# Moving two of four PSUM evictions from ScalarE to VectorE, and moving once-a-batch stages to other slots, in a causal attention kernel

## The chip, the cores and the metric

The kernel runs on 1 core of one Trainium2 chip. The metric is device time in microseconds (us) of the whole program. The kernel before takes 3825.32 us, the median of 3 runs (3816.24 to 3826.53).

## The reference

```python
x = L0_attn_x                                   # 8 x 512 x 128, float32
h = _layernorm(x) * (1 + ca) + sa               # per-batch modulation
x = x + ga * attn(h)                            # 16 heads of 8, 512 tokens, rope, causal softmax
h = _layernorm(x) * (1 + cb) + sb
x = x + gb * ffn_stack(h)                       # 6 layers: windowed attention + gated FFN

# attn(h):
q, k, v = heads(x @ Wq.T), heads(x @ Wk.T), heads(x @ Wv.T)
q, k = _apply_rope(q, k, cos, sin)
scores = einsum('bhqd,bhkd->bhqk', q, k) / sqrt(8) + causal_mask
out = einsum('bhqk,bhkd->bhqd', softmax(scores), v)
return out.reshape(B, S, 128) @ Wo.T
```

The change is in the causal attention, the first part of the program ("the causal half", `part_a` in the code). The 6-layer stack behind it (`part_b`) and the output (`part_c`) are the same in both kernels, and start when the causal half has ended.

## The kernel before, in words

The causal half works through 8 batches. A batch has 16 heads, taken in 4 groups of 4, so there are 32 groups. In each group, the queries and keys of the 4 heads are laid out on 128 partitions, 32 partitions to a head (8 rows in use for the head, two float32r parts of each, and in row 0 of the block the constant one of `one`, which lets a product add the row maximum).

Each engine's program is written as a loop over slots `s`, and each stage of the work is given a slot number: TensorE does the fills of stage X at slot X_AT (+11 per group, or +44 per batch), and the engine that empties the bank does it at X_AT+1 or later. A group has 11 slots (`PER`), a batch 44. All engines run through the slots in the same order, but each waits only for the semaphores of the instruction that comes next, so the order within a slot and the distance in slots between a producer and its consumer set who waits for whom. In each slot TensorE does:

- the fills of the general bank of that slot: there are 2 such banks, `gen0` and `gen1`, used in turn by all stages together, in the order of the list `gen_order`. `begin` (L360 on) makes a fill wait until the fill but one before it has been emptied. The stages of every group are stackq, stackk, stack2 (4 heads' queries, keys, and queries with their maximum), turn and back (the output turned, and the denominators turned back). In places modulo 11 they are at 3, 5, 2, 9 and 4. The stages that come once a batch are h (normed input turned), q, qr, k, kr (projections, plain and rotated), v, y (output projection), yt and h2. In places modulo 44 they are at 5, 10, 12, 13, 15, 20, 31, 34 and 43; so h shares a slot with stackk, k with stack2, kr with back, v and y with turn.
- one step of `scores` (L420, L421): scores by query into one of 3 banks `tm`. VectorE takes their negated row maximum (L737). The step of slot s waits (`need(pe, max_d, u - 2)`) until the maximum of slot s-3 has been taken.
- one step of `scores_by_key` (L435, L437), for a group 16 slots before, into one of 2 banks `km`. ScalarE takes the exponential (L587). The step waits for the exponential of two slots before.
- at four of eleven places one `weigh` (L451), which multiplies the exponentials with the values into `po`. ScalarE copies `po` to `oT` (L578) at place 7, and turn at place 9 reads it.

The stack of keys (stackk, place 5) is emptied in four pieces of 32 partitions (L549), one per head, each into its own column block of `kG` (3 of these homes). All four are done by ScalarE, one in each slot at the places 6, 7, 8 and 9, ahead of that slot's exponential. Only the fourth counts up `g_act`, which is what the scores of the next group (place 0) wait for and what the fill after next in the banks `gen` waits for.

VectorE multiplies q, qr, k, kr with the rope tables (L699) one slot after each fill, takes the maxima, takes part in turn, back and yt, and does two layernorms per batch: "h" in five parts at the places 40, 42, 44, 46, 48 of the batch, and "h2" in five parts at 35 to 39. Each of these parts stands ahead of the maximum of its slot. GpSimd adds the rope halves (L602) and takes the low parts (L607).

Of the kernel before, what the change touches and what calls it, by code (L numbers as in the profile page):

```python
# [193 lines left out]
    return g if r == 0 and 0 <= g < NG else None  # L194


H_AT, Q_AT, QR_AT, K_AT, KR_AT, V_AT = -39, -34, -32, -31, -29, -24
STACKQ_AT, STACKK_AT, STACK2_AT, TURN_AT, BACK_AT = -8, -6, 13, 31, 37
WEIGH_AFTER = 1
Q_HOMES, K_HOMES = 2, 3  # L200
Y_AT, YT_AT, H2_AT = 75, 78, 87


def gen_order():
# [31 lines left out]
def part_a(nc, t_in, alloc, need, x_attended, resT, ident, masks, mod, vecs):  # L236
# [3 lines left out]
    with ctx:  # L240
        sb, ps, sem = alloc(ctx)
# [10 lines left out]
        one = sb("one", [P, 1])  # L252
# [38 lines left out]
        mod_p = sem("mod_p"); mod_e = sem("mod_e"); mod_d = sem("mod_d"); sel_d = sem("sel_d")  # L291
        rot_w = sem("rot_w"); vec_e = sem("vec_e"); vec_z = sem("vec_z"); clear_d = sem("clear_d"); clear_k = sem("clear_k"); wo_p = sem("wo_p"); wo_d = sem("wo_d")
        st = sem("st"); passed = sem("passed"); rstd_d = sem("rstd_d"); nrm = sem("nrm"); ahead_d = sem("ahead_d"); after_d = sem("after_d")
        g_fill = sem("g_fill"); g_act = sem("g_act"); g_dve = sem("g_dve")
        rope_a = sem("rope_a"); hi_d = sem("hi_d"); lo_d = sem("lo_d")
        tm_full = sem("tm_full"); max_d = sem("max_d"); km_full = sem("km_full"); exp_d = sem("exp_d")
        w_done = sem("w_done"); o_out = sem("o_out"); wide_d = sem("wide_d")
# [34 lines left out]
        def _(pe):  # L332
# [25 lines left out]
            def begin(name, k):  # L358

                i = GEN[name, k]  # L360
                if i >= 2:
                    user = GEN_LIST[i - 2]
                    if user[0] in BY_VECTOR:
                        pe.wait_ge(g_dve, GEN_DVE[user] + 1)
                    else:
                        pe.wait_ge(g_act, GEN_ACT[user] + 1)
                return gen[i % 2]

            def four_turns(bank, src):
# [40 lines left out]
            def scores(u):  # L410

                gr, i = divmod(u, PER)
                j, hh, n = ROWS[i]
                if i == 0:
                    pe.wait_ge(g_act, GEN_ACT["stackk", gr] + 1)
                need(pe, max_d, u - 2)
                pe.sem_inc(pe_passed, 1)
                width = (j + 1) * P
                bank = tm[u % 3][:, 0:n * width].rearrange("p (h w) -> p h w", h=n)
                nc.tensor.matmul(bank, qG[:, gr % Q_HOMES, j * P:width], kG[:, gr % K_HOMES, hh:hh + n, 0:width], start=True, stop=False)  # L420
                nc.tensor.matmul(bank[:, :, j * P:width], ident_r, causal_mask.rearrange("p (o k) -> p o k", o=1).broadcast_to(  # L421
                    [P, n, P]), start=False, stop=True).then_inc(tm_full, 1)
# [86 lines left out]
        @block.scalar  # L509
        def _(act):  # L510
            act.wait_ge(tr_w, 1)
            nc.scalar.activation(wT[:, 0:4, :], tm[0][:, :].rearrange("p (i f) -> p i f", i=4), ACT.Copy).then_inc(ev_w, 1)
            nc.scalar.activation(cT[:, :], tm[1][:, 0:BATCH], ACT.Silu).then_inc(silu_d, 1)
            act.wait_ge(loaded, NLOAD)
            nc.scalar.activation(sel[:, :, :], sel_raw[:, :, :], ACT.Copy).then_inc(sel_d, 1)
            nc.scalar.activation(mask_r[:, :], masks[:, 2 * KEYS:2 * KEYS + 3 * P], ACT.Copy).then_inc(sel_d, 1)
            act.wait_ge(wo_p, 1)
            nc.scalar.activation(wo_rows[:, :, :], tm[0][:, :].rearrange("p (i f) -> p i f", i=4), ACT.Copy).then_inc(wo_d, 1)
            act.wait_ge(clear_d, 3)

            def filled(name, k):
                act.wait_ge(g_fill, GEN[name, k] + 1)
                return gbank(name, k)

            for s in A_SLOTS:
                b = batch_at(s, H_AT + 1)
                if b is not None:
                    bank = filled("h", b)
                    act.wait_ge(ahead_d, b + 1)
                    nc.scalar.activation(hT[:, :], bank[:, :], ACT.Identity, bias=ahead_mod[:, 0:1],  # L530
                                         scale=ahead_mod[:, 1:2]).then_inc(g_act, 1)
                b = batch_at(s, V_AT + 1)
                if b is not None:
                    bank = filled("v", b)
                    need(act, w_done, 16 * (b - 1))
                    nc.scalar.activation(values[:, b % 2, :, :, 0:A_HDIM], bank[:, :].rearrange(
                        "p (t h d) -> p t h d", t=TILES, h=A_HEADS), ACT.Copy).then_inc(g_act, 1)
                gr = group_at(s, STACKQ_AT + 1)
                if gr is not None:
                    bank = filled("stackq", gr)  # L540
                    nc.scalar.activation(qG[:, gr % Q_HOMES, :], bank[:, :], ACT.Copy).then_inc(g_act, 1)
                for hh in range(4):
                    gr = group_at(s, STACKK_AT + 1 + hh)
                    if gr is not None:
                        bank = filled("stackk", gr)
                        if gr < K_HOMES:
                            act.wait_ge(clear_k, gr + 1)
                        r = slice(32 * hh, 32 * hh + 32)
                        last = nc.scalar.activation(kG[r, gr % K_HOMES, hh, :], bank[r, :], ACT.Identity, bias=one[r, 0:1])  # L549
                        if hh == 3:  # L550
                            last.then_inc(g_act, 1)
                gr = group_at(s, STACK2_AT + 1)
                if gr is not None:
                    bank = filled("stack2", gr)
                    nc.scalar.activation(q2[:, gr % 2, :], bank[:, :], ACT.Copy).then_inc(g_act, 1)
                b = batch_at(s, Y_AT + 1)
                if b is not None:
                    bank = filled("y", b)
                    act.wait_ge(after_d, b + 1)
                    nc.scalar.activation(yT[:, :], bank[:, :], ACT.Copy, scale=after_mod[:, 0:1]).then_inc(g_act, 1)  # L560
                b = batch_at(s, H2_AT + 1)
                if b is not None:
                    bank = filled("h2", b)
                    nc.scalar.activation(resT[:, b, :], bank[:, :], ACT.Identity, bias=after_mod[:, 1:2],
                                         scale=after_mod[:, 2:3]).then_inc(g_act, 1)
                for c, off in ((0, Q_AT + 5), (1, K_AT + 5)):
                    b = batch_at(s, off)
                    if b is not None:
                        act.wait_ge(rope_a, 2 * b + c + 1)
                        if b >= 2:  # L570
                            act.wait_ge(g_fill, GEN["stack2", GROUPS * (b - 1) - 1] + 1)
                        nc.scalar.activation(qk_hi[:, b % 2, c, :], rot1[:, c, :], ACT.Copy).then_inc(hi_d, 1)
                gr = group_at(s, LAG + PER + WEIGH_AFTER + 1)
                if gr is not None:
                    act.wait_ge(w_done, 4 * gr + 4)
                    if gr >= 2:
                        act.wait_ge(g_dve, GEN_DVE["back", gr - 2] + 1)
                    nc.scalar.activation(oT[:, gr % 2, :], po[:, :], ACT.Copy).then_inc(o_out, 1)  # L578
                u = s - LAG
                if 0 <= u < NU:  # L580
                    gr, i = divmod(u, PER)
                    k, hh, n = KEYED[i]
                    if hh == 0:
                        need(act, w_done, 4 * gr + k - 2)
                    act.wait_ge(km_full, u + 1)
                    width = TOKENS - k * P
                    nc.scalar.activation(probT[:, (4 * gr + k) % 3, hh:hh + n, 0:width],  # L587
                                         km[u % 2][:, 0:n * width].rearrange("p (h w) -> p h w", h=n), ACT.Exp).then_inc(exp_d, 1)

        @block.gpsimd  # L590
        def _(pool):
# [5 lines left out]
            for s in A_SLOTS:  # L597
                for c, off in ((0, QR_AT + 2), (1, KR_AT + 2)):
                    b = batch_at(s, off)
                    if b is not None:  # L600
                        pool.wait_ge(g_dve, GEN_DVE[("qr", "kr")[c], b] + 1)
                        nc.gpsimd.tensor_tensor(rot1[:, c, :], rot1[:, c, :], rot2[:, c, :], ALU.add).then_inc(rope_a, 1)  # L602
                for c, off in ((0, Q_AT + 6), (1, K_AT + 6)):
                    b = batch_at(s, off)
                    if b is not None:
                        pool.wait_ge(hi_d, 2 * b + c + 1)
                        nc.gpsimd.tensor_tensor(qk_lo[:, b % 2, c, :], rot1[:, c, :], qk_hi[:, b % 2, c, :].bitcast(f32),  # L607
                                                ALU.subtract).then_inc(lo_d, 1)
# [9 lines left out]
        def _(dve):  # L618
# [64 lines left out]
            for s in A_SLOTS:  # L683
# [10 lines left out]
                for c, r, off in ((0, 0, Q_AT), (0, 1, QR_AT), (1, 0, K_AT), (1, 1, KR_AT)):  # L694
                    b = batch_at(s, off + 1)
                    if b is not None:
                        bank = filled(("q", "qr", "k", "kr")[2 * c + r], b)
                        need(dve, lo_d, 2 * (b - 1) + c + 1)
                        nc.vector.tensor_tensor((rot1, rot2)[r][:, c, :], bank[:, :], rope[:, 2 * c + r, :],  # L699
                                                ALU.mult).then_inc(g_dve, 1)  # L700
                gr = group_at(s, TURN_AT + 1)
                if gr is not None:
                    bank = filled("turn", gr)
# [827 lines left out]
```

## Time and profile before

| | |
|---|---|
| median of 3 runs | 3825.32 us |
| the profiled execution: its own time, its span | 3833.82 us, 3832.0 us |
| causal half, setup (0 to 49 us) | TensorE busy 18.25 us |
| causal half, loop (49 to 660 us) | 611 us; busy TensorE 542.35, VectorE 309.24, ScalarE 349.43, GpSimd 55.49 us |
| tail of the causal half (660 to 673 us) | 13 us |
| 6-layer stack and output (673 to 3832 us) | 3159 us |

The span is the time from the first to the last instruction of one profiled execution; the time of that execution has 1.82 us around it. Busy times are the union of an engine's instructions in a stretch. "Idle before" an instruction is the time its engine stood still, and the arrow names what ended the wait. PEclk is the TensorE clock that the chip granted: 1.00 is 2.4 GHz, 0.50 is 1.2 GHz.

### The profile page before, as it was taken

To read this page: it belongs to the slowest core of one execution; us is meant where nothing else is said; L and a number is where in the kernel's file an instruction comes from. 1 tells how busy PE (TensorE), PEld (TensorE's weight loads), DVE (VectorE), ACT (ScalarE), POOL (GpSimd) and SP (SyncE) were. 2 spreads that over 40 slices of the span, in tenths; PEclk is the share of its full clock that TensorE was granted. 3 is DMA by queue.
4 is the path that set the end of the run, shared out by engine and by line. 5 is a ranking of instruction groups with operands and counts; after the bars stand their busy time and mean duration, and the time that the engine had idled before them with its cause. 6 is when DMAs were issued, how large, how long until landed. Compare 5 with 4: busy or idle time off the path is not lost. (4 is left out here: it accounts for less than half of the span.)

```text
span 3832.0 us, 147280 instructions
## 1 busy us (share of the span) xinstructions
PE 3621.4 (95%) x64322; PEld 2756.7 (72%) x64322; DVE 3100.3 (81%) x4927; ACT 2455.5 (64%) x3855; POOL 2310.7 (60%) x1367
## 2 busy tenths in 40 slices
PE   6888888599999999999999999999999999999996
PEld 4666665477777777777777777777777777777774
DVE  4554454699988899989899989988899998889893
ACT  4555555367666667666667666666666766666663
POOL 1001000677777677777677777776777777777771
PEclk9999999799999999999999999999999999999998
DMA  1000000222222222222222222212222222221112
GB/s 56 4 4 4 4 7 7 64 54 56 54 56 54 68 54 56 54 56 60 61 54 56 54 63 62 56 53 56 54 68 54 56 54 54 57 57 52 52 52 70
DMA packets 122998, 188.79 MB, mean 49 GB/s; under 512 B 25054, under 2 KB 44278, under 8 KB 122108
## 3 DMA queue, kind: packets, MB, share of 16 engines
q1 hardware_dynamic: 122364, 179.36, 17.3%
q8 instruction: 517, 8.47, 0.9%
q14 instruction: 117, 0.96, 0.1%
HBM read 24.08 MB, written 4.19 MB: 7 GB/s over the span
## 5 line engine op out<-in xcount | busy, mean ns | idle before, releaser
L1308 POOL TENSOR_TENSOR rc<-rc,rnorm 128x1024 f32<-128x1024 f32 x384 | 731.4, 1905 | 394.5 <-DVE rnorm L170 377.4
L1302 POOL TENSOR_TENSOR rc<-rc,rs 128x1024 f32<-128x1024 f32 x384 | 910.6, 2371 | 7.2 <-DVE rs L1367 3.6
L1343 POOL TENSOR_TENSOR prob_b<-prob_b,rinv 128x1024 f32<-128x1024 f32 x192 | 365.4, 1903 | 358.3 <-DVE rinv L1448 358.2
L1361 DVE TENSOR_TENSOR rc<-proj,rope_b 128x1024 f32<-128x1024 f32 x384 | 465.6, 1212 | 87.1 <-ACT squares L1165 85.9
L1165 ACT ACTIVATE squares<-proj 128x1024 f32<-128x1024 f32 x384 | 392.7, 1023 | 181.5 <-PE proj L917 178.0
L1008 PEld LDWEIGHTS ring<-pT,vmoved 64*64 64x64 f32 x18432 | 380.3, 135 | 136.1 <-issue 136.1
L1367 DVE TENSOR_TENSOR rs<-proj,rope_b 128x1024 f32<-128x1024 f32 x384 | 466.1, 1214 | 0.0
L1375 DVE TENSOR_REDUCE sums<-squares 128x16 f32<-128x1024 f32 x384 | 463.9, 1208 | 0.0
L954 PEld LDWEIGHTS ring<-ident,rc 128*128 128x128 f32 x3072 | 361.5, 141 | 138.9 <-issue 43.5
L737 DVE TENSOR_REDUCE negmax<-tm 128x1 f32<-128x384 f32 (+3 forms) x352 | 222.3, 639 | 285.3 <-PE tm L421 285.0
L954 PE MATMUL ring<-ident,rc 128*128 128x128 f32 x3072 | 428.7, 277 | 12.2 <-POOL rc L1308 9.7
L1008 PE MATMUL ring<-pT,vmoved 64*64 64x32 f32 x18432 | 404.8, 221 | 25.2 <-issue 23.6
L1008 PE MATMUL ring<-pT,vown 64*64 64x32 f32 x6144 | 378.2, 220 | 6.1 <-issue 6.1
L1156 ACT ACTIVATE qT<-ring 128x512 f32<-128x512 f32 x384 | 228.3, 595 | 204.9 <-PE ring L954 204.9
L915 PE MATMUL proj<-wqkv_hi,xa_hi 128*128 128x512 f32 x768 | 330.3, 430 | 28.2 <-POOL xa_lo L1284 21.5
L1023 PE MATMUL proj<-oT_b,wo 128*128 128x256 f32 x1536 | 351.8, 383 | 2.0 <-issue 2.0
L587 ACT ACTIVATE probT<-km 128x512 f32<-128x512 f32 (+1 forms) x352 | 195.1, 557 | 241.7 <-PE km L437 236.5
L1156 ACT ACTIVATE vown<-ring 128x512 f32<-128x512 f32 x384 | 229.4, 598 | 178.2 <-PE ring L917 168.0
L1008 PEld LDWEIGHTS ring<-pT,vown 64*64 64x64 f32 x6144 | 332.5, 135 | 6.8 <-issue 6.8
L1156 ACT ACTIVATE pT<-ring 128x512 f32<-128x512 f32 x384 | 218.4, 595 | 183.7 <-PE ring L987 182.6
L974 PE MATMUL scr<-kT,qT 64*32 64x64 f32 x24576 | 332.8, 224 | 1.6 <-issue 1.3
L1156 ACT ACTIVATE kT<-ring 128x512 f32<-128x512 f32 x384 | 228.6, 595 | 157.6 <-PE ring L954 157.5
(172 smaller groups left out, 8027.4 us busy)
## 6 DMA issues: line engine op xcount, KB each, us to landing
vmoved<-vown SPq DMA_DIRECT2D x576, 128.0 KB
vmoved<-vown SPq DMA_DIRECT2D x192, 192.0 KB
vmoved<-vown SPq DMA_DIRECT2D x576, 64.0 KB
wqkv_raw<-in_L_ffn_Wqkv SPq DMA_DIRECT2D x40, 192.0 KB, 3.4
wo<-in_L_ffn_Wo SPq DMA_DIRECT2D x6, 512.0 KB, 4.8
x_attended<-xtok SPq DMA_DIRECT2D x8, 256.0 KB, 2.0
xtok_c<-x_attended SPq DMA_DIRECT2D x8, 256.0 KB, 4.4
out<-xtok_c SPq DMA_DIRECT2D x8, 256.0 KB, 2.8
```

Source lines behind the costliest of these rows:

```text
L954: last = nc.tensor.transpose(bank[:, p * P:(p + 1) * P], rc[:, k % 2, c, o:o + P], ident[:, :])
L974: last = nc.tensor.matmul(scr[32 * w:32 * w + 32, s, p, :], qT[rows, p, 32 * w:32 * w + 32], kT[rows, p, j * P + 32 * w:j * P + 32 * w + K ...
L1008: last[i] = nc.tensor.matmul(banks[i][64 * b:64 * b + 64, p, 32 * odd:32 * odd + 32], v[64 * s:64 * s + 64, :], pT[64 * s:64 * s + 64, p, ...
L1023: last = nc.tensor.matmul(bank[:, HALVES[half]], wo[:, p, :], oT[:, p, HALVES[half]], start=(p == 0), stop=(p == PAIRS - 1))
L1156: nc.scalar.activation(dst, src, ACT.Copy).then_inc(ring_free, 1)
L1165: nc.scalar.activation(squares[:, c, :], proj[c][:, :], ACT.Square).then_inc(sq_done, 1)
L1302: nc.gpsimd.tensor_tensor(rc[:, k % 2, c, :], rc[:, k % 2, c, :], rs[:, c, :], ALU.add).then_inc(add_done, 1)
L1308: nc.gpsimd.tensor_tensor(dst, dst, rnorm[:, k % 2, c * HEADS:(c + 1) * HEADS].rearrange("p (h o) -> p h o", o=1).broadcast_to([P, HEADS, ...
L1343: nc.gpsimd.tensor_tensor(pr, pr, rinv[:, :, :].rearrange("p q (s o) -> p q s o", o=1).broadcast_to([P, PAIRS, 2, KEYS]), ALU.mult).then_i ...
L1361: nc.vector.tensor_tensor(rc[:, k % 2, c, :].rearrange("p (h d) -> p h d", h=HEADS), proj[c][:, :].rearrange("p (h d) -> p h d", h=HEADS), ...
L1367: nc.vector.tensor_tensor(rs[:, c, :].rearrange("p (h s d) -> p h s d", h=HEADS, s=2), src[:, :, ::-1, :], tab.broadcast_to([P, HEADS, 2, ...
L1375: nc.vector.tensor_reduce(sums[:, c * HEADS:(c + 1) * HEADS], squares[:, c, :].rearrange("p (h d) -> p h d", h=HEADS), AX.X, ALU.add).then ...
```

## The change

Three things are changed. First, ScalarE does only the first two of the four evictions of a stack of keys, at the places 6 and 7; VectorE does the other two at the same places, as a `tensor_scalar` that adds the per-partition scalar `one`, and counts a semaphore of its own, `k_half`. Whoever waited for ScalarE's fourth eviction now waits for ScalarE's second and for `k_half`. Second, the batch stages get other slots: h from place 5 to 7, qr from 12 to 11, k from 13 to 12, kr from 15 to 18, v from 20 to 21, y from 31 to 32. None of them is in a slot with a stage of the groups any more. Third, the steps that follow the rotation are counted from the rotated projection: the high part (L572) goes from 15 and 18 to 14 and 21, the low part (L607) from 16 and 19 to 15 and 22.

```diff
-H_AT, Q_AT, QR_AT, K_AT, KR_AT, V_AT = -39, -34, -32, -31, -29, -24
+H_AT, Q_AT, QR_AT, K_AT, KR_AT, V_AT = -37, -34, -33, -32, -26, -23
...
-Y_AT, YT_AT, H2_AT = 75, 78, 87
+Y_AT, YT_AT, H2_AT = 76, 78, 87
...
                     else:
                         pe.wait_ge(g_act, GEN_ACT[user] + 1)
+                    if user[0] == "stackk":
+                        pe.wait_ge(k_half, 2 * user[1] + 2)
...
                 if i == 0:
                     pe.wait_ge(g_act, GEN_ACT["stackk", gr] + 1)
+                    pe.wait_ge(k_half, 2 * gr + 2)
...
-                for hh in range(4):
+                for hh in range(2):
                     gr = group_at(s, STACKK_AT + 1 + hh)
...
-                        if hh == 3:
+                        if hh == 1:
                             last.then_inc(g_act, 1)
...
-                for c, off in ((0, Q_AT + 5), (1, K_AT + 5)):
+                for c, off in ((0, QR_AT + 3), (1, KR_AT + 3)):
...
-                for c, off in ((0, Q_AT + 6), (1, K_AT + 6)):
+                for c, off in ((0, QR_AT + 4), (1, KR_AT + 4)):
...
+                for hh in (2, 3):
+                    gr = group_at(s, STACKK_AT - 1 + hh)
+                    if gr is not None:
+                        bank = filled("stackk", gr)
+                        if gr < K_HOMES:
+                            dve.wait_ge(clear_k, gr + 1)
+                        r = slice(32 * hh, 32 * hh + 32)
+                        nc.vector.tensor_scalar(kG[r, gr % K_HOMES, hh, :], bank[r, :], one[r, 0:1], None, ALU.add).then_inc(k_half, 1)
```

How the order of the instructions changes is shown at three places. The line numbers of the kernel after the change are 2 to 11 higher for the same statement.

ScalarE, a group without batch stages; `kG<-gen` is an eviction of keys, `probT<-km` an exponential, `oT<-po` the copy that turn needs. Before:

```order
L587 ACTIVATE probT<-km 128x4x128
L587 ACTIVATE probT<-km 128x512
L549 ACTIVATE kG<-gen,one 32x512
L587 ACTIVATE probT<-km 128x512
L549 ACTIVATE kG<-gen,one 32x512
L578 ACTIVATE oT<-po 128x512
L587 ACTIVATE probT<-km 128x512
L549 ACTIVATE kG<-gen,one 32x512
L587 ACTIVATE probT<-km 128x512
L549 ACTIVATE kG<-gen,one 32x512
```

The same place after the change:

```order
L590 ACTIVATE probT<-km 128x4x128
L590 ACTIVATE probT<-km 128x512
L552 ACTIVATE kG<-gen,one 32x512
L590 ACTIVATE probT<-km 128x512
L552 ACTIVATE kG<-gen,one 32x512
L581 ACTIVATE oT<-po 128x512
L590 ACTIVATE probT<-km 128x512 x2
```

The two evictions behind `oT` are gone; the two ahead of it, and `oT` itself, stand where they stood.

TensorE, the slot in which the values of a batch are projected (`gen<-wT,hT`), beside turn (`gen<-ident,oT`). Before:

```order
L437 MATMUL km<-mask_r 128x128
L383 MATMUL gen<-wT,hT 128x128 x4
L371 MATMUL gen<-ident,oT 128x128 x4
L420 MATMUL tm<-kG,qG 128x512
L421 MATMUL tm<-mask_r 128x128
L435 MATMUL km<-q,kG 128x384
```

After, behind turn and one step of the scores:

```order
L438 MATMUL km<-q,kG 128x384
L440 MATMUL km<-mask_r 128x128
L385 MATMUL gen<-wT,hT 128x128 x4
L423 MATMUL tm<-kG,qG 128x512
L424 MATMUL tm<-mask_r 128x128
```

The projection of the values moved behind turn, into the next slot; the output projection y (L488) did the same.

VectorE, the stretch of a batch in which both layernorms are at work (`xn` is the last part of one, `stats` the first of the other, `negmax<-tm` the maxima of the scores). Before:

```order
L737 TENSOR_REDUCE negmax<-tm 128x1
L676 TENSOR_SCALAR xn<-xtok,mv,rstd 128x128 x4
L737 TENSOR_REDUCE negmax<-tm 128x1
L656 BN_STATS stats<-xtok 128x6 x4
L737 TENSOR_REDUCE negmax<-tm 128x1 x2
L688 COPY ahead_mod<-mod 128x2
L661 BN_AGGR mv<-stats 128x2 x4
```

After:

```order
L748 TENSOR_REDUCE negmax<-tm 128x1
L711 TENSOR_SCALAR kG<-gen,one 32x512
L679 TENSOR_SCALAR xn<-xtok,mv,rstd 128x128 x4
L748 TENSOR_REDUCE negmax<-tm 128x1
L659 BN_STATS stats<-xtok 128x6 x4
L711 TENSOR_SCALAR kG<-gen,one 32x512
L748 TENSOR_REDUCE negmax<-tm 128x1 x2
```

One eviction of keys stands ahead of each of two maxima, where VectorE also has the parts of the two norms.

## Rows read from the trace of the kernel before

**Rows 1.** The page's first line: the span of the profiled execution

```profile
span 3832.0 us, 147280 instructions
```

**Rows 2.** Busy time by stretch: from:to, length, PE, PEld, DVE, ACT, POOL, PEclk, DMA share, GB/s

```profile
49.00:660.00 611.00, 542.35 (x3542) 383.17 (x3541) 309.24 (x745) 349.43 (x614) 55.49 (x60) 0.97 0.01 4
279.27:357.74 78.47, 68.98 (x449) 48.66 (x448) 40.21 (x101) 44.43 (x78) 7.58 (x8) 0.98 0.01 4
279.27:303.44 24.17, 20.04 (x119) 13.89 (x117) 9.62 (x16) 11.95 (x21) 5.74 (x5) 0.93 0.00 1
323.29:339.89 16.60, 15.17 (x113) 11.33 (x112) 13.27 (x50) 10.88 (x19) 0.61 (x1) 1.00 0.04 17
590.19:604.99 14.80, 14.32 (x104) 10.54 (x103) 7.58 (x13) 10.16 (x18) 0.61 (x1) 1.00 0.00 1
604.99:626.53 21.54, 19.53 (x112) 12.66 (x111) 7.58 (x14) 10.84 (x19) 0.61 (x1) 0.92 0.00 1
```

**Rows 3.** Waits of TensorE, 40 to 660 us: total, times, longest

```profile
PE gen L371 <- ACT kG L549: 21.4, 12, 2.4
PE gen L390 <- DVE rot L699: 12.6, 20, 1.4
PE gen L488 <- ACT kG L549: 12.5, 7, 1.8
PE gen L371 <- ACT oT L578: 8.7, 24, 0.8
PE gen L378 <- ACT kG L549: 7.2, 6, 1.2
PE tm L420 <- ACT kG L549: 2.9, 1, 2.9
PE km L435 <- ACT probT L587: 2.3, 8, 0.5
PE gen L371 <- DVE xn L676: 1.2, 1, 1.2
```

**Rows 4.** Waits of TensorE in one batch's 44 slots, 279.3 to 357.7 us

```profile
PE gen L371 <- ACT kG L549: 3.6, 2, 2.4
PE gen L488 <- ACT kG L549: 1.8, 1, 1.8
PE gen L390 <- DVE rot L699: 1.8, 3, 1.0
PE gen L378 <- ACT kG L549: 1.2, 1, 1.2
PE gen L371 <- ACT oT L578: 1.1, 3, 0.6
```

**Rows 5.** Groups by line and shape (count | busy us, mean ns); the first: min/median/max ns

```profile
L549 ACT ACTIVATE kG<-gen,one x128: 662/679/682, 44.3 to 617.9; 32x512 fp32r<-32x512 f32 x128
...
L737 DVE TENSOR_REDUCE negmax<-tm 128x1 f32<-128x384 f32 x128 | 71.1, 556 | 81.3 <-PE tm L421 81.3
...
L699 DVE TENSOR_TENSOR rot<-gen,rope 128x512 f32<-128x512 f32 x28 | 19.1, 680 | 0.0
```

**Rows 6.** Timeline (start, us), VectorE and TensorE where both norms work

```profile
331.81 1.11 DVE L676 TENSOR_SCALAR xn<-xtok,mv,rstd 128x128 f32<-128x128 f32 x4
...
333.30 0.86 DVE L656 BATCH_NORM_STATS2 stats<-xtok 128x6 f32<-128x128 f32 x4
334.07 1.27 DVE L737 TENSOR_REDUCE negmax<-tm 128x1 f32<-128x512 f32 x2
...
337.80 0.47 PE L420 MATMUL tm<-kG,qG 128*128 128x512 f32 x1
```

**Rows 7.** Timeline of a group without batch stages

```profile
599.06 0.56 DVE L737 TENSOR_REDUCE negmax<-tm 128x1 f32<-128x384 f32 x1 [0.79 <-PE tm L421]
...
600.25 1.37 DVE L737 TENSOR_REDUCE negmax<-tm 128x1 f32<-128x512 f32 x2 [0.64 <-PE tm L421]
...
602.50 0.44 PE L420 MATMUL tm<-kG,qG 128*128 128x512 f32 x1
```

More of the change, by code:

```diff
@@ L293, in part_a @@
         st = sem("st"); passed = sem("passed"); rstd_d = sem("rstd_d"); nrm = sem("nrm"); ahead_d = sem("ahead_d"); after_d = sem("after_d")
-        g_fill = sem("g_fill"); g_act = sem("g_act"); g_dve = sem("g_dve")
+        g_fill = sem("g_fill"); g_act = sem("g_act"); g_dve = sem("g_dve"); k_half = sem("k_half")
         rope_a = sem("rope_a"); hi_d = sem("hi_d"); lo_d = sem("lo_d")
```

## The prediction

> **What bounds the kernel now.** The times of the stretches come first, since the change touches only the causal half. Of the 3832.0 us of the span [rows 1], its loop is 611.00 us, and TensorE is busy for 542.35 of them; ScalarE (349.43) and VectorE (309.24) have room [rows 2]. TensorE is the engine to follow, and its time in the loop has three parts: its work, its idle time of 611.00 - 542.35 = 68.7 us, and what a lower clock costs. All that the change can give back is in the last two. The 3159 us behind the causal half are its successor in time, with the same program, so every microsecond saved in the loop should be a microsecond of the whole.
>
> Next, the waits of TensorE [rows 3]. ScalarE's evictions of keys end 21.4 + 12.5 + 7.2 = 41.1 us of waits in front of fills of the general banks (turn and h2, y, q) and 2.9 us once, ahead of the first scores. VectorE's rope products end 12.6 us. The copy of `po` ends 8.7 us, the exponentials 2.3 us. No maximum of VectorE ends any wait of TensorE: that is the resource that the change will draw on.
>
> Then one batch. Its 44 slots take 78.47 us, with TensorE busy for 68.98, so 9.5 us idle [rows 2], and the waits of that stretch add up to the same: 3.6 + 1.8 + 1.8 + 1.2 + 1.1 = 9.5 [rows 4]. Over the loop the fills of L371 waited 21.4 us in 12 waits for kG, against 3.6 in 2 here [rows 3, 4]: six batches do the same. A group without batch stages takes 14.80 us with 0.48 us idle [rows 2], so the trouble lies in the batch stages. The reason can be read from the code: with two general banks each fill waits for the fill but one before it. Turn at place 9 normally follows stackk at place 5 as the very next fill, and waits for back. When v, y, q or h2 comes between or behind, the fill after next behind stackk falls on place 9 or 10, and stackk's last piece leaves ScalarE at place 9. TensorE is at most two slots ahead of ScalarE's exponentials, so it must then stand still until ScalarE has caught up. The rope products are the same thing in small: qr is at 12, emptied at 13, and stack2 at 13 wants its bank; likewise k with stackq, kr with stackk.
>
> Last the clock. The group that holds the wait of 2.4 us has a granted clock of 0.93 over 24.17 us, all others of the batch 1.00 [rows 2]. That is one stretch at 1.2 GHz, right after the longest idle time of the batch, and it costs (1 - 0.93) x 24.17 = 1.7 us. The group with the last y has 0.92 over 21.54 us, again 1.7 us, behind an idle time of 1.8.
>
> **The change part by part, for one batch.**
>
> - Evictions of keys. ScalarE's second piece is at place 7 and VectorE's last too, where the fourth was at 9. The earliest fill that asks for stackk's bank is at 9 (turn, behind h at 7), then 10 (q, y, h2). TensorE at slot 9 already needed the exponential of slot 7 in slot 9's own work, and the scores of 9 need the maximum of 6; so both releases are behind it or nearly so. All waits on kG go: -6.6 us [rows 4]. What is late next at turn is `oT`, which stays at place 7 behind the same two evictions: 0.2 us in each group, as in the groups that wait for it today.
> - qr, k, kr, v in slots of their own. Each product is now one slot ahead of the fill that needs its bank, and stands ahead of a maximum that takes 0.68 us in a slot of some 1.3 us. The three waits go: -1.8 us [rows 4].
> - `oT`. Before, 1.1 us in three waits, one of them 0.6 because the eviction of h (place 6) and a high part (place 18, the 7 of its group) stood ahead of the copy. Both move behind it. Four waits of the short kind, (1.1 - 0.6) / 2 = 0.25 or a little less: 0.9 us, so -0.2. The eviction of h is now at 8, ahead of an exponential, where an eviction of keys stands today, and the waits for exponentials are 2.3 / 8 = 0.3 us each [rows 3]: +0.3.
> - Clock. With idle times of at most 0.3 us left, I expect no stretch at 1.2 GHz: -1.7.
> - y, yt, h2, low parts: moved by one slot or to an idle GpSimd (55.49 us busy in 611 [rows 2]): 0.
>
> Sum: -6.6 - 1.8 - 0.2 + 0.3 - 1.7 = -10.0 us per batch, 60 us over six batches. Outside these six: the other rope waits, 12.6 - 6 x 1.8 = 1.8; the last y 1.8 and its clock 1.7; the one wait for `xn` of 1.2, as h is two slots later; the first keys, emptied by two engines, where VectorE also has a part of a norm between its two pieces, so only 0.5 of 2.9; waits on exponentials 1.0 of 2.3 [rows 3]. Together 8.0. Total -68 us.
>
> What it costs on VectorE: 64 evictions. The trace has no `tensor_scalar` from a general bank. The nearest rows are a 512-wide product from such a bank, 680 ns, and a 384-wide maximum, 556 ns; ScalarE's form of the same eviction takes 679 [rows 5]. I take 0.68, with 0.56 and 0.8 as ends. That is 64 x 0.68 = 44 us on an engine that idles half the time. Queued behind them is the maximum of the same slot, and TensorE waits for it three slots later. In a group without batch stages VectorE idled 0.79 and 0.64 us ahead of the two maxima in question [rows 7], so 1.36 us of evictions fit in 1.43 us of idle time: 0. The tight place is the one with both norms, where VectorE is busy for 13.27 of 16.60 us [rows 2]; it will have 14.6 in about 15.4. Replayed from [rows 6] with the evictions put in: the first eviction from 331.81 to 332.49, `xn` to 333.6, its maximum to 334.15, the statistics to 334.95, the second eviction to 335.6, its maximum to 336.2. The scores that need this one stood at 337.80 and come 1.2 us earlier, at 336.6. Room: 0.4 us. It should pass, but with so little I take 2 us off for all batches together. So -66 us.
>
> The profiled execution took 3833.82 us, so the sum gives 3767.8. That execution is 8.5 us above the median of the runs shown (3825.32), and I expect the same offset: 3759 us.
>
> A place where the pages speak. In this trace no general bank is read by two engines at once; after the change ScalarE reads partitions 0 to 63 and VectorE 64 to 127 of one bank at the same places. The Trainium skill, "PSUM — Partial Sum Buffer", section "PSUM bank collisions raise a hardware error", quotes AWS that no two engines may be in one bank within a partition in the same cycle, and says that different quadrants of one bank run clean. By that the two evictions keep their length, and the sum stands; no run so far shows it. As for the clock, [rows 2] show 0.93 only in the group with the longest idle time. "TensorE: Matmul & The Clock Gate", section "A second HAM failure mode: psum-queue depth-cycling", of the Trainium skill tells that short idle times between groups of matmuls are enough to make the clock swing. By that rule a stretch at 1.2 GHz could stay although the long wait is gone; that is rival 2.
>
> **Rivals.**
>
> 1. VectorE becomes late. In the stretch with both norms the evictions take 0.2 us more each, or its small instructions lose more than I replayed; TensorE waits for maxima. For it: 14.6 of 15.4 us busy. Against: 0.4 us of room, and two or three slots of distance. Price: 2 to 2.5 us per batch, 17 us in all: 3759 + 17 = 3776.
> 2. The clock drops all the same, at another place of the batch. For it: six batches show it at the same place, so some pattern of work as well as the wait may be behind it; the wait of 1.8 us at y costs nothing in six batches and 1.7 us in the last. Against: no group with waits under 1.3 us has it. Price: 8 x 1.7 = 13.6: 3773.
> 3. ScalarE takes the place of its own wait: TensorE, no longer held at the general banks, is held at the exponentials or at `oT` in every group, 1 us more in each. For it: both waits are there today whenever kG does not wait. Against: ScalarE is busy for 10.16 of 14.80 us and gets 1.36 less to do [rows 2]. Price: 32 us: 3791.
> 4. The moved stages do nothing: what TensorE waits for in a batch is really the sum of ScalarE's work, and the waits reappear at the next gate. Against: only 44.43 of 78.47 us are ScalarE's. It would give 3815 to 3825.
> 5. Slower. One mechanism: VectorE's eviction from a bank that ScalarE reads takes so long that the maxima are late in every group. In [rows 7] the second of the maxima concerned, at 600.25, ends at about 600.94 and is needed at 602.50, 1.56 us later; with d for an eviction it comes 2d - 1.43 later. TensorE begins to wait at d = 1.5 us. To undo 66 us and lose 11.5 more, it must wait 77 / 32 = 2.4 us per group, which needs d = (1.43 + 1.56 + 2.4) / 2 = 2.7 us, four times the nearest row. It would give 3837 or more.
>
> **How the numbers follow.** Forecast 0.64, with 3747 to 3768 as its own range: the low end if every wait of these rows and the clock went, 3825.3 - 78, the high end with all small terms against me. Rival 1 0.14, rival 2 0.09, rival 3 0.06, rival 4 0.04, rival 5 0.03. The range 3746 to 3785 holds the first three with their spread and leaves out rivals 3 to 5, and a little below. About 0.3%, 11.5 us, is what can be told from no change. Faster: 0.64 + 0.14 + 0.09 + 0.06 = 0.93. Same 0.04, slower 0.03.
>
> **What the profile after would show.** Right: no wait of TensorE for kG or the rope products, a batch of 68 to 69 us instead of 78.5, waits for `oT` of about 0.2 us in each group, PEclk 1.00 throughout the middle of the loop, VectorE's evictions at 0.68 us, the stretch from the end of the loop on as long as before. Wrong: a row of TensorE's scores waiting for a maximum (rival 1), PEclk under 1.00 in every batch (rival 2), waits for exponentials above 10 us in sum (rival 3), or evictions far over 0.8 us (rival 5).

## The result, and the profile after

The changed kernel takes 3742.69 us (median of 4 runs, 3739.59 to 3750.11) against 3825.93 us before (4 runs, 3816.24 to 3834.54): a ratio of 0.978, interval 0.9765 to 0.9796, or 83 us less. The forecast was 3759 with 3746 as its low end. The direction and the mechanism were right, the size was 17 us short, and the measured time lies 3 us below the range.

The page after the change, first line, to hold against [rows 1]; the execution took 3750.11 us.

```profile
span 3748.0 us, 147316 instructions
```

Where the 84.0 us between the two spans lie can be read from when the stack behind the causal half begins (its first instruction on GpSimd): 673.9 us before, 590.0 after. The rest takes 3158.1 and 3158.0 us. So in these two executions the whole difference is in the causal half. Its middle, six batches from the same point to the same point, before and then after (from:to, length, PE, PEld, DVE, ACT, POOL, PEclk, DMA share, GB/s):

```profile
104.30:575.38 471.08, 414.04 (x2690) 292.09 (x2688) 239.45 (x591) 266.65 (x468) 45.47 (x48) 0.98 0.01 4
```

```profile
96.80:494.81 398.01, 393.92 (x2689) 283.53 (x2688) 278.98 (x644) 232.46 (x420) 45.41 (x49) 1.00 0.02 5
```

471.08 - 398.01 = 73.1 us, 12.2 per batch where 10.0 were forecast. TensorE's idle time fell by 57.04 - 4.09 = 53.0 us; its busy time fell too, by 20.1 us, for the same matmuls. Half of that is the clock, the other half is what the forecast missed. One batch, the two of its groups that held the longest wait and both norms, then the first group without batch stages and the one with the last y, which answer to the last five of [rows 2]:

```profile
229.62:296.03 66.41, 65.70 (x450) 47.26 (x449) 46.71 (x111) 38.75 (x71) 7.50 (x8) 1.00 0.02 5
...
246.00:262.57 16.57, 16.57 (x116) 12.18 (x115) 11.04 (x18) 10.49 (x19) 5.11 (x5) 1.00 0.01 1
...
280.39:296.03 15.64, 15.26 (x113) 11.35 (x112) 13.89 (x48) 9.42 (x17) 0.00 (x0) 1.00 0.05 18
494.81:509.20 14.39, 14.15 (x105) 10.52 (x104) 9.10 (x15) 8.77 (x17) 0.61 (x1) 1.00 0.00 1
523.58:541.57 17.99, 17.58 (x112) 12.04 (x111) 9.42 (x16) 9.39 (x17) 0.61 (x1) 1.00 0.00 1
```

The group that took 24.17 us before takes 16.57 now, with no idle time and at the full clock. The waits of TensorE over the six batches (97 to 495 us) are one row where [rows 4] had five for each batch:

```profile
PE gen L373 <- ACT oT L581: 2.8, 12, 0.2
```

No wait on `kG`, none on the rope products, and `oT` in only two groups of four. Ahead of the six batches the forecast's first sign of being wrong did appear once, a step of the scores that waits for a maximum of VectorE (window 40 to 660 us):

```profile
PE tm L423 <- DVE negmax L748: 0.6, 1, 0.6
```

It is in the first batch, where the kernel before has no such wait. The evictions on VectorE (duration in ns, min/median/max), to hold against [rows 5]:

```profile
L711 DVE TENSOR_SCALAR kG<-gen,one x64: 747/754/761, 41.9 to 533.1; 32x512 fp32r<-32x512 f32 x64
```

The place with both norms, to hold against [rows 6], which has the same stretch 42 us later (start, duration, engine, line, operation, count, idle before):

```profile
289.01 0.75 DVE L711 TENSOR_SCALAR kG<-gen,one 32x512 fp32r<-32x512 f32 x1
...
289.22 0.66 ACT L552 ACTIVATE kG<-gen,one 32x512 fp32r<-32x512 f32 x1
...
289.80 1.12 DVE L679 TENSOR_SCALAR xn<-xtok,mv,rstd 128x128 f32<-128x128 f32 x4
...
291.42 0.86 DVE L659 BATCH_NORM_STATS2 stats<-xtok 128x6 f32<-128x128 f32 x4
...
292.31 0.76 DVE L711 TENSOR_SCALAR kG<-gen,one 32x512 fp32r<-32x512 f32 x1
...
293.10 1.29 DVE L748 TENSOR_REDUCE negmax<-tm 128x1 f32<-128x512 f32 x2
293.17 0.63 PE L373 MATMUL gen<-ident,xn 128*128 128x128 f32 x4
...
293.94 0.47 PE L423 MATMUL tm<-kG,qG 128*128 128x512 f32 x1
```

The scores at 293.94 need the first of the two maxima that begin at 293.10 and would otherwise start 0.36 us after the transposes; here they follow by 0.77 (0.36 in the last kernel below). VectorE is late by some 0.4 us once in a batch, and no row says so: the end of the transposes is modelled at 293.80, and the 0.14 us behind it are under what the views count as a wait.

### The profile page after: what moved, and what is told of

Read it like the earlier page. It is cut to its first block and busy times, and to the rows that moved or that the text cites. A ratio compares the mean times of both kernels' runs of the same rounds, so it can differ in the third digit from the quotient of the medians.

```text
span 3748.0 us, 147316 instructions
## 1 busy us (share of the span) xinstructions
PE 3597.6 (96%) x64322; PEld 2745.5 (73%) x64322; DVE 3149.5 (84%) x4991; ACT 2410.4 (64%) x3791; POOL 2310.4 (62%) x1367
## 5 line engine op out<-in xcount | busy, mean ns | idle before, releaser
L1034 PEld LDWEIGHTS proj<-oT_b,wo 128*128 128x128 f32 x1536 | 291.5, 192 | 46.8 <-issue 4.1
```

Of the source, the lines that this page charges most:

```text
L1034: last = nc.tensor.matmul(bank[:, HALVES[half]], wo[:, p, :], oT[:, p, HALVES[half]], start=(p == 0), stop=(p == PAIRS - 1))
```

## The experiments

Each was run with its own profile. The stack behind the causal half took between 3150 and 3168 us in these profiled executions, though its program is the same in all of them. That spread is larger than most effects here, so the experiments are read from the length of a batch in the loop (groups 12 to 15 of 32: 78.47 us before, 66.41 after) and from the end of the causal half (673.9 and 590.0). The batch repeats well: the changed kernel run again gave 66.43, and its six batches 398.04 us in place of 398.01. The end of the causal half came out at 590.0 again, but its parts outside the six batches moved by 1 us each (the first scores 0.9 us later, the stretch behind the last scores 1.0 us shorter), so a difference of 1 us in it tells nothing.

### One half of the change at a time

```diff
-H_AT, Q_AT, QR_AT, K_AT, KR_AT, V_AT = -37, -34, -33, -32, -26, -23
+H_AT, Q_AT, QR_AT, K_AT, KR_AT, V_AT = -39, -34, -32, -31, -29, -24
-Y_AT, YT_AT, H2_AT = 76, 78, 87
+Y_AT, YT_AT, H2_AT = 75, 78, 87
```

> The change's evictions (two of four on VectorE, all at places 6 and 7) with every batch stage in its slot of before. Theory A (the waits on kG come from the last eviction leaving at place 9; the stretch at 1.2 GHz comes from the longest of them): waits of TensorE on kG gone, PEclk 1.00 in the middle of the loop, the three waits on rope products per batch stay at 1.8 us of idle time, and the copy oT keeps a wait of 0.6 us in the group of h. Of 12.1 us saved per batch about 8.5 remain: batch about 70 us, whole kernel about 3768 us. Rival B (the waits come from batch stages sharing a slot with group stages): kG's waits are replaced by others at turn and y of the same size, batch above 75 us, whole kernel above 3800.

3775.66 us (3763.03 to 3779.33; ratio 0.9871, 0.9847 to 0.9894), batch 70.15, causal half to 613.8 us. Its waits in one batch (241 to 311 us), and the stretch of that batch:

```profile
PE gen L392 <- DVE rot L702: 1.8, 3, 1.0
PE gen L373 <- ACT oT L581: 1.1, 3, 0.7
```

```profile
241.19:311.33 70.14, 67.00 (x449) 47.31 (x448) 46.39 (x111) 38.38 (x71) 7.60 (x8) 1.00 0.01 5
```

Theory A: the evictions alone give 8.3 of the 12.1 us, all waits on kG are gone and with them the stretch at 1.2 GHz. Rival B falls. The causal half is 24 us longer than after the change, as 3768 supposes; the 8 us over it are spread of the rest.

The other half, built on the kernel before, with h in its old place and the high and low parts counted from the rotated projection as after the change:

```diff
-H_AT, Q_AT, QR_AT, K_AT, KR_AT, V_AT = -39, -34, -32, -31, -29, -24
+H_AT, Q_AT, QR_AT, K_AT, KR_AT, V_AT = -39, -34, -33, -32, -26, -23
-Y_AT, YT_AT, H2_AT = 75, 78, 87
+Y_AT, YT_AT, H2_AT = 76, 78, 87
```

> All four evictions on ScalarE at places 6 to 9 as before, and the new slots of qr, k, kr, v and y; h stays in its slot of before (place 5). Theory A: rope waits gone, but turn behind kr, q, y and h2 still wait for kG: 4 to 6 us of idle time per batch; batch about 73 us, whole kernel 3785 to 3795 us. Rival B (shared slots are the cause): no wait on kG above 1 us per batch, batch 68 us or less, 3755 us or less.

3800.41 us (3794.49 to 3806.94; 0.9943, 0.9927 to 0.996), batch 74.95, causal half to 648.5 us. Waits in one batch (251 to 326 us), and the group behind which they are longest:

```profile
PE gen L371 <- ACT kG L549: 3.2, 2, 2.0
PE gen L488 <- ACT kG L549: 1.2, 1, 1.2
PE gen L378 <- ACT kG L549: 1.2, 1, 1.2
PE gen L371 <- ACT oT L578: 1.1, 3, 0.7
```

```profile
269.72:290.11 20.39, 18.37 (x116) 13.18 (x115) 9.53 (x16) 11.97 (x21) 5.65 (x5) 0.92 0.00 1
```

The waits on kG are 5.6 us, as theory A has it, and rival B falls here too; the batch is 2 us longer than expected since the clock still drops behind the wait of 2.0 us. The slots alone give 3.5 us, and 8.3 + 3.5 = 11.8 is nearly the 12.1 of both. But this kernel leaves h in its old place, which costs 0.9 us by itself in the changed kernel (below), so the parts are not simply a sum. What can be said: on top of the evictions, all the new slots together give 70.15 - 66.41 = 3.7 us.

### Is it the place of the last eviction, or the engine?

```diff
-                for hh in range(2):
-                    gr = group_at(s, STACKK_AT + 1 + hh)
+                for hh in range(4):
+                    gr = group_at(s, STACKK_AT + 1 + hh // 2)
```

with VectorE's evictions and `k_half` taken out.

> All slots as after the change, but ScalarE does all four evictions, two at place 6 and two at place 7. It tells whether it is the place of the last eviction alone that matters, or that ScalarE is relieved. If the place alone: waits as after the change, 3743 us. If ScalarE's queue matters: the copy oT, which stands behind the evictions at place 7, comes about 1.4 us later in each group, and turn and the exponentials wait for it; 1 to 1.5 us in each of 32 groups, whole kernel 3775 to 3790 us.

3778.07 us (3776.4 to 3785.67; 0.9888, 0.9874 to 0.9903), batch 70.63. ScalarE at one group, then TensorE's waits in one batch:

```profile
290.61 1.37 ACT L549 ACTIVATE kG<-gen,one 32x512 fp32r<-32x512 f32 x2
292.00 0.60 ACT L578 ACTIVATE oT<-po 128x512 f32<-128x512 f32 x1
```

```profile
PE gen L371 <- ACT oT L578: 4.7, 4, 1.5
```

Both answers hold in part. An earlier last eviction frees the banks also when ScalarE does it: with the new slots, the batch falls from 78.47 to 70.63 us. Without VectorE the copy `oT` comes later, and the waits for it grow from 0.5 to 4.7 us per batch, while VectorE's hidden lateness of 0.4 us is gone: the four slots with turn are 4.64 us longer than after the change, slot 43 is 0.45 us shorter. That is the 4.2 us between the two batches. VectorE's share in the change is to keep the queue in front of `oT` short.

### The rope stages

```diff
-H_AT, Q_AT, QR_AT, K_AT, KR_AT, V_AT = -37, -34, -33, -32, -26, -23
+H_AT, Q_AT, QR_AT, K_AT, KR_AT, V_AT = -37, -34, -32, -31, -29, -23
```

> As after the change, with qr, k and kr back in the slots of before (12, 13, 15). The three waits on rope products come back with 1.8 us of idle time per batch. Theory C (a wait costs TensorE more than its idle row shows, some 0.25 us each, because the first matmul behind it starts with nothing loaded ahead): the batch grows by 2.5 us to 68.9, whole kernel about 3761. Rival D (idle rows are the whole cost, and the rest of what the change saved came from other neighbours of the stages): the batch grows by 1.8 us to 68.2, whole kernel about 3756.

3775.86 us (3770.15 to 3780.29; 0.9878, 0.9863 to 0.9893), batch 70.14, causal half to 614.9. The waits in one batch (240.7 to 311 us):

```profile
PE gen L392 <- DVE rot L702: 1.8, 3, 1.0
PE gen L373 <- ACT oT L581: 1.4, 3, 0.9
```

The batch grew by 3.7 us, more than either theory said, because the high part came back ahead of `oT` and added a wait of 0.9 us, which I had not put into the expectation. Taken slot by slot (from one mask matmul of the scores to the next), the slots of the rope stages grew by 2.66 us for 1.78 us of idle rows, and the slot with turn by 1.07 for 0.90. That is what theory C says: 0.29 and 0.17 us for each wait beside its row. By slots alone it could also be that the moved stages cost more beside other neighbours, as h does below; the start times below leave that out, since they compare the same three matmuls.

The batch of 70.14 us is also that of the evictions-only kernel (70.15), which has h, v and y in their old slots besides. So moving h gives nothing as long as the rope stages are not moved.

The two short stretches are of the first two kernels; PEld is the load of the weights. Before, with a wait of 0.51 us for the rope product:

```profile
290.06 0.45 PE L437 MATMUL km<-mask_r 128*128 128x512 f32 x1
291.02 0.19 PEld L390 LDWEIGHTS gen<-qk_hi,sel 128*128 128x128 f32 x1 [0.83 <-DVE rot L699]
291.02 0.50 PE L390 MATMUL gen<-qk_hi,sel 128*128 128x512 f32 x1 [0.51 <-DVE rot L699]
291.36 0.39 PE L391 MATMUL gen<-qk_lo,sel 128*128 128x512 f32 x1
```

After, the same three matmuls in a group without a wait:

```profile
501.17 0.45 PE L440 MATMUL km<-mask_r 128*128 128x512 f32 x1
501.22 0.19 PEld L392 LDWEIGHTS gen<-qk_hi,sel 128*128 128x128 f32 x1
501.46 0.39 PE L392 MATMUL gen<-qk_hi,sel 128*128 128x512 f32 x1
501.68 0.39 PE L393 MATMUL gen<-qk_lo,sel 128*128 128x512 f32 x1
```

From the first start to the third it is 1.30 us against 0.51: 0.79 us for a row of 0.51. Without a wait the next matmul starts 0.16 us before the end that is shown for the one ahead of it (501.17 + 0.45 = 501.62), while idle time is counted only from that end. And the matmul behind the wait takes 0.34 us to the next start instead of 0.22: its weights begin to load with it, at 291.02, where they are loaded 0.24 us ahead of it without a wait (501.22 and 501.46). Together 0.28 us beside the row, and rival D falls.

### h, and v with y

As after the change, with `H_AT` back at -39:

> As after the change, with h (the four transposes of the normed input) back at place 5, in front of stackk. Its eviction returns to place 6, ahead of the copy oT. Waits: oT in that group 0.6 us instead of none. If a wait costs its idle row and 0.15 to 0.3 us more, and the transposes themselves cost 0.8 us in front of stackk against 0.4 us alone (slots 5 and 7 of the batch, before against after): batch 66.4 + 0.8 + 0.4 = 67.6 us, whole kernel 8 us longer. If the transposes cost the same in both places: batch 67.2 us. No effect: 66.4 us.

Batch 67.33, causal half to 597.6 us (one run, 3755.86 us). In front of stackk the transposes cost 0.80 us, alone 0.39; the wait for `oT` returned (0.65) and its slot grew by 0.80; one slot of q shrank by 0.27. Sum +0.93, where 1.2 were expected: the shrinking slot was not foreseen.

As after the change, with `V_AT` back at -24 and `Y_AT` at 75:

> As after the change, with v and y back at 20 and 31, in front of and behind turn, and the evictions of keys still at places 6 and 7. Theory A (only the late eviction made these two wait): no wait on kG, batch 66.4 us within 0.3, whole kernel as after the change. Rival B (sharing the slot with turn costs by itself): turn or y waits for what stands between, batch 68 us or more, whole kernel 10 us longer.

Batch 66.47, causal half to 591.0 us. Theory A: once the keys leave by place 7, it does not matter that v and y share a slot with turn. The single run took 3761.16 us, 11 us more than the profiled run of the changed kernel, with 1.0 of them in the causal half and 10.1 in the stack behind it, where the programs do not differ: read by its total time, this experiment would have told the opposite.

### How much room VectorE has

Each of VectorE's evictions done twice, and three times:

```diff
+                        nc.vector.tensor_scalar(spare0[r, :], bank[r, :], one[r, 0:1], None, ALU.add)
                         nc.vector.tensor_scalar(kG[r, gr % K_HOMES, hh, :], bank[r, :], one[r, 0:1], None, ALU.add).then_inc(k_half, 1)
```

> As after the change, and VectorE does each of its evictions twice (the first time into a tile that nobody reads), so each costs 1.51 us where it costs 0.754. By the room that was worked out from the trace before (two maxima absorb 1.43 us and the second of them has 1.56 us to spare) a group without batch stages has 2 x 1.51 - 1.43 - 1.56 = 0.03 us of waiting: none to be seen. Where both norms work, slot 43, which has a hidden wait of 0.44 us, gets 1.5 us more. Batch about 67.9 us, whole kernel about 3754. If VectorE has less room than that, waits of the scores for maxima in every group.

3764.54 us (3759.5 to 3769.57; 0.9815, 0.978 to 0.9851), batch 68.24, causal half to 602.5. A group without batch stages takes 14.54 us instead of 14.38; slot 43 takes 2.81 instead of 1.47. Both as worked out, to 0.2 us. In the batch two other slots are 0.4 us longer each and one is 0.3 us shorter.

> As e7, with each eviction done three times, 2.26 us for each: this is beyond the point of 1.5 us from which rival 5 was to decide. By the same working 4.52 - 1.43 - 1.56 = 1.5 us of waiting in every group, and some 3.4 us where both norms work: batch 66.4 + 3 x 1.5 + 3.4 = 74.3 us, whole kernel about 3805. Waits of TensorE's scores (L426) on VectorE's maxima appear in every group.

3820.48 us (3814.39 to 3826.1; 0.9965, 0.9946 to 0.9984), batch 75.32, causal half to 652.7. Two groups without batch stages (554 to 586 us), and the first of them:

```profile
PE tm L425 <- DVE negmax L752: 2.6, 2, 1.3
```

```profile
554.15:570.02 15.87, 14.33 (x105) 10.53 (x103) 11.68 (x19) 8.76 (x17) 0.61 (x1) 1.00 0.00 1
```

15.87 - 14.38 = 1.49 us, where 1.5 was expected. So rival 5 was a real mechanism with its point at about 1.5 us per eviction; at the 0.754 us that they take it does not begin. The six batches differ here, from 72.2 us at PEclk 1.00 (the last, which has no norm of h) and 73.5 us at 0.99 to 75.3 us at 0.95, where 74.3 was expected. The expectation had left out the clock; without it the lengths would lie below what was worked out. Nor do the waits for maxima appear in every group: in the six batches they are 1.7 us in six waits, and 18.2 us in twelve waits of transposes are put down to nothing that the profile shows.

### What was left: oT, and the hidden wait

The copy `oT` moved ahead of the eviction of keys in its slot; in the second kernel the norm of h one slot later as well:

```diff
-                    b = batch_at(s, -48 + 2 * part)
+                    b = batch_at(s, -47 + 2 * part)
```

> As after the change, with the copy oT moved ahead of the eviction of keys in ScalarE's slot of place 7. Turn's wait of 0.24 us goes in the 18 groups that have it. If a wait costs 0.15 to 0.3 us beside its idle row, each of them gives 0.4 us: 18 x 0.4 = 7 us, batch 65.6 us, whole kernel 7 us under the changed one, 3736. If idle rows are the whole cost: 18 x 0.24 = 4 us, batch 65.9. If the copy waits for the last weigh and holds up the eviction and the exponential behind it, the exponentials take over and nothing is gained: batch 66.4.

3744.88 us (3743.4 to 3753.37; ratio to before 0.9789, 0.9775 to 0.9802), batch 66.18, causal half to 587.8. No wait of TensorE is left in the six batches, but the causal half gains 2.2 us, 1.7 of them in the six batches, and not 7. The slot with turn lost 0.42 us for a wait of 0.24, which is theory C again; 0.18 came back in the next slot, where the exponentials are now what comes last, too short to be shown as a wait; and in the group with both norms VectorE's lateness took all of it.

> As e9, with the five parts of the norm of h one slot later (41, 43, 45, 47, 49), so that its statistics no longer stand in a slot with VectorE's eviction of keys. If slot 43's 0.44 us (1.47 against 1.03 us in the last batch, which has no such norm) is VectorE being late with the maximum of slot 40, it goes: batch 0.4 us under that of e9, about 65.2 us, whole kernel 3 us under e9. If not: as e9.

3739.53 us (3735.46 to 3742.58; ratio to before 0.9769, 0.9756 to 0.9782), batch 65.48, causal half to 583.0 us. The group that had the hidden wait:

```profile
278.25:293.19 14.94, 14.94 (x112) 11.31 (x111) 13.25 (x44) 9.41 (x17) 0.00 (x0) 1.00 0.05 19
```

14.94 us with no idle time, where it was 15.64 and, with `oT` first, still 15.64. So the hidden wait was VectorE's; its 0.44 us went, and with it came through most of what `oT` had given in that group (0.42 us, of which 0.18 came back in the next slot as in the other group). The 0.7 us are more than the 0.4 expected for this reason. The causal half is 7.0 us shorter than after the change, 5.2 of them in the six batches.

> The changed kernel once more, beside e9 and e10 on the same chip: 3743 us, batch 66.4 us.

3749.39 us (3742.81 to 3755.05; ratio to before 0.9795, 0.978 to 0.981). The two versions differ by 7 us in the causal half, but their intervals still touch, so by total time the last kernel is only probably the fastest.

## Why the prediction was right and wrong

- What bounds the kernel, and that a microsecond of the loop is one of the whole: right, but its closeness is luck. The stack behind takes the same time to 0.1 us in these two profiles; in the changed kernel run again it took 3153.0 us, 5 us less. So the 84.0 us of the causal half and the 83.2 us between the medians agree within that spread, no better.
- Waits on kG, -6.6 us per batch: right. With the rope waits and the rest, idle time per batch went from 9.5 to 66.41 - 65.70 = 0.7 us, 8.8 less, where my terms were 6.6 + 1.8 + 0.2 - 0.3 = 8.3. I had `oT` at 0.9 us where 0.5 is left, and a wait for the exponentials of 0.3 that did not come.
- Clock, -1.7: right. The stretch at 1.2 GHz before can be seen by itself, here 3.25 us of it, all busy; at the full clock it would take half as long, 1.6 us less:

```profile
298.82:302.07 3.25, 3.25 (x12) 2.86 (x12) 1.25 (x3) 0.97 (x2) 0.61 (x1) 0.50 0.03 5
```

After the change PEclk is 1.00 over the six batches. Rival 2 did not come. The evictions-only kernel has no wait above 1.1 us and no drop; with the slots alone the wait of 2.0 us and the drop stayed.

- The step that failed is the sum itself: "the waits of that stretch add up to the same", taken as what their going is worth. Idle 8.8 + clock 1.7 = 10.5 us; 12.1 were measured (12.2 as the mean of the six). The missing 1.6 us per batch, 10 us over six batches, were in the busy time. Each wait cost 0.15 to 0.3 us beside its row wherever it could be taken alone (0.29 and 0.28 for the rope products, 0.15 to 0.19 for `oT` in four kernels), and eight of ten in a batch went, an estimate of some 1.6 us; h costs 0.4 us less where no fill follows it; VectorE's hidden lateness gives 0.4 back. For the waits on kG the surcharge was not taken alone.
- The terms outside the six batches: 8.0 forecast, 84.0 - 73.1 = 10.9 measured, with 7.5 us of it before the first of them, where I had about 4.5. Of the 7.5, the first scores start 2.8 us earlier (47.8 and 45.0 us). The slots of the first batch take 4.7 us less: TensorE's idle time in them fell by 3.1 us, and its busy time by 1.7 at a PEclk of 0.92 before and 0.95 after, about all of it clock. The sum had neither an earlier start, beyond 0.5 us for the first keys, nor this clock. Part of it is chance: the changed kernel run again starts its first scores at 45.9.
- VectorE: 0.754 us for an eviction, not 0.68; room of 0.4 us in the tight place, all used and 0.4 us more. From the start of the first eviction to the end of the maximum in question the replay had 4.4 us, and the trace gives 4.8 (from 289.01 to 293.79, the end of the first of the two maxima); TensorE was ready for it at 4.5, where the replay had 4.8. The 2 us taken off in all were about right (0.44 x 6 = 2.6). The working of rival 5's point held to 0.2 us in the groups without batch stages of both kernels that tested it.
- Two engines in one bank: the rows at 289.01 and 289.22 overlap, with 0.75 and 0.66 us, the second as long as ScalarE's evictions were alone. Of the 64 pairs 55 overlap; in these VectorE's part takes 750 ns in the median and ScalarE's 678, in the nine others 759 and 682. So reading one bank side by side lengthened neither. The Trainium skill, "PSUM — Partial Sum Buffer", section "PSUM bank collisions raise a hardware error", says that accesses to different quadrants of one bank run clean, and the trace agrees; that the lengths stay was the prediction's own step, and it held.
- The range: its low end was drawn from "if every wait of these rows and the clock went". It left out that the rows might be less than the waits cost. In sum: 73.1 - 60 = 13.1 for the batches, 2.9 outside them and the 2 us taken off, 18.0 us = 84.0 - 66.

The move of v and y, which the change makes too, is worth 0.06 us per batch.

## What to carry to other kernels

Where two banks are used in turn by many stages, look at which fill comes after next behind the slowest eviction: here, pulling its last piece forward two slots, with half of the evictions on another engine, gave 8.3 us per batch, and giving single stages their own slots 3.5 to 3.7 us. In this kernel a wait of TensorE is worth its idle row and some 0.15 to 0.3 us more, best read as the distance between the same two starts with and without the wait. Where a program is long and only a part is changed, compare the end of that part: the unchanged rest varied by 18 us from run to run.

## What the runs showed of the hardware that was not expected

- A `tensor_scalar` on VectorE, 32 x 512 from PSUM into float32r with a per-partition scalar, takes 0.754 us. A two-input product 128 x 512 from PSUM takes 0.680, and ScalarE's form of the same eviction 0.679. Neither form got longer when both engines read one bank at once, in different partitions.
- What TensorE had done before its clock fell from 2.4 to 1.2 GHz in the loop: in each of the six batches before the change a wait of 2.35 us, with the slots alone one of 2.0 us. With each of VectorE's evictions done three times, four waits of 2.06 us had a fall of the clock during them or behind them, and a fifth, at 404.6 us, had none. Waits of 1.5 us in most groups (ScalarE by place 7) left it at 2.4 GHz through the six batches. The wait of 1.8 us at y, before the change, came without a drop in six groups and with one in the last; with the slots alone one group dropped behind waits of no more than 1.2 us. So there is no length of a wait that decides by itself.
